# Halves of 128 slots with an expert each, constants of the attention tiles from GpSimd, and unpaced scatters of the first set, in a macaron block on one core

## The reference

```python
x = x + 0.5 * ffn(layernorm(x))       # mixture of experts, 8 experts, 2 per token
x = x + attention(layernorm(x))       # 16 heads of 8 features, causal, softmax
x = x + 0.5 * ffn(layernorm(x))

# ffn: probs = softmax(flat @ gate_w.T); the 2 best experts of a token, weights scaled to sum 1
h1 = einsum('nd,ehd->neh', flat, w1)
h3 = einsum('nd,ehd->neh', flat, w3)
y = einsum('neh,edh->ned', silu(h1) * h3, w2)     # 256 hidden features an expert
out = einsum('ned,ne->nd', y, combine)            # combine is zero outside the 2 experts
```

## Time and profile before

| | |
|---|---|
| median of 3 runs | 617.2 us (616.16 to 620.45) |
| the profiled execution's own time | 616.21 us |
| its span, first to last instruction | 613.7 us |
| mean granted TensorE clock | 0.973 |
| busy, share of the span: PE, PEld, DVE, ACT, POOL | 84%, 68%, 61%, 51%, 42% |
| matmul records | 7286 |
| DMA | 72.15 MB, 124981 packets, mean 118 GB/s |

### The profile page before, as it was taken

One profiled execution on the slowest core, in us unless ns is written; L12 is line 12 of the kernel. 1 busy time (PEld: TensorE's weight loads), 2 busy tenths in 40 slices (PEclk: granted clock), 3 DMA queues, 4 the chain that ended last, 5 costly groups with the idle time before them and its releaser, 6 DMA issues.

```text
span 613.7 us, 19025 instructions
## 1 busy us (share of the span) xinstructions
PE 514.6 (84%) x7286; PEld 416.7 (68%) x7286; DVE 373.7 (61%) x995; ACT 310.0 (51%) x597; POOL 257.5 (42%) x322
## 2 busy tenths in 40 slices
PE   2779859999998588888889886769689899999995
PEld 1667848889987355555556554546368789989994
DVE  5633933343355868989899988666356333356665
ACT  5843523344334256666666764555554234345543
POOL 7565364630563133433341111454614530555562
PEclk9999998999999589999999999998999999999999
DMA  9991297646965213746213110311134656543232
GB/s 269 307 323 35 81 277 118 137 129 146 165 153 142 80 42 95 198 126 179 90 38 97 38 55 3 123 34 33 32 79 97 138 133 130 140 131 98 67 89 56
DMA packets 124981, 72.15 MB, mean 118 GB/s; under 512 B 51936, under 2 KB 118752, under 8 KB 124896
## 3 DMA queue, kind: packets, MB, share of 16 engines
q1 hardware_dynamic: 117984, 56.78, 35.4%
q0 software_dynamic: 6912, 14.17, 9.3%
HBM read 18.88 MB, written 34.87 MB: 88 GB/s over the span
## 4 chain that ended last, share of the span: by engine, by line
PE 35%; DVE 17%; issue 4%; ACT 3%; another core or an unknown queue 2%; DMA 1%; DVEq 1%; POOL 0%; ACTq 0%; POOLq 0%
PE bank L1629 8%; DVE negmax L1310 7%; PE bank L1510 5%; PE bank L1512 5%; PE bank L1511 4%; PE bank L1742 2%; PE bank L1805 2%; ACT pt L958 2%; PE bank L1820 2%; PE bank L1772 2%; PE bank L1808 1%; PE bank L1759 1%; DVE rden L1327 1%; PE bank L1522 1%
## 5 line engine op out<-in xcount | busy, mean ns | idle before, releaser
L1197 DVE SCALAR_TENSOR_TENSOR pt<-bank,pt 128x512 f32<-128x512 f32 x122 | 84.2, 691 | 152.6 <-PE bank L1512 69.4
L708 POOL DMA_INDIRECT yg<-sorted_y,row x108 | 104.2, 965 | 146.9 <-PE bank L1629 64.2
L958 ACT ACTIVATE pt<-bank 128x768 f32<-128x768 f32 x128 | 103.8, 811 | 87.7 <-PE bank L1781 81.8
L694 POOL DMA_INDIRECT sorted_x<-xs,row x108 | 106.2, 984 | 90.0 <-DVE pt L1197 32.3
L1629 PE MATMUL bank<-w,pt 128*128 (+1 forms) x976 | 131.8, 277 | 7.6 <-issue 5.4
L1629 PEld LDWEIGHTS bank<-w,pt 128*128 128x128 f32 x976 | 119.7, 192 | 13.6 <-issue 10.0
L1310 DVE TENSOR_REDUCE negmax<-bank 128x10 f32<-128x640 f32 x128 | 104.1, 817 | 30.6 <-PE bank L1759 26.7
L841 ACT ACTIVATE pt<-bank 128x512 f32<-128x512 f32 x122 | 73.2, 600 | 57.3 <-PE bank L1512 38.9
L1742 PE MATMUL bank<-zc 63*64 63x64 f16 (+3 forms) x1024 | 44.4, 251 | 28.0 <-DVE negmax L1310 22.9
L849 ACT ACTIVATE yb<-bank 128x256 f32<-128x256 f32 x82 | 31.5, 384 | 67.9 <-PE bank L1629 43.2
L1742 PEld LDWEIGHTS bank<-zc 63*64 63x64 f16 x1024 | 19.4, 108 | 55.7 <-DVE negmax L1310 37.0
(11 more groups left out here) (171 smaller groups left out, 1014.1 us busy)
## 6 DMA issues: line engine op xcount, KB each, us to landing
sorted_y<-yb SPq DMA_DIRECT2D x82, 128.0 KB
zc<-qk_rows SPq DMA_DIRECT2D x96, 64.0 KB
sorted_x<-zeros SPq DMA_DIRECT2D x2, 2944.0 KB
qk_rows<-qksplit SPq DMA_DIRECT2D x8, 512.0 KB
sorted_x<-zeros SPq DMA_DIRECT2D x1, 2432.0 KB, 11.3
sorted_x<-zeros SPq DMA_DIRECT2D x1, 2176.0 KB, 10.2
X<-x_in SPq DMA_DIRECT2D x8, 256.0 KB, 5.3
zc<-w_up SPq DMA_DIRECT2D x8, 256.0 KB, 7.1
```

The source lines that it names most:

```text
L694: ps.indirect_dma_start(out=sorted_x[s], out_offset=bass.IndirectOffsetOnAxis(ap=row[:, s, k, t:t + 1], axis=0), in_=xs[:, R0[s] + t, :], ...
L708: ps.indirect_dma_start(out=yg[:, a % D_YG, k, :], out_offset=None, in_=sorted_y[s], in_offset=bass.IndirectOffsetOnAxis(ap=row[:, s, k, t ...
L958: s_.activation(pt[:, hg, (u % 2) * 768:(u % 2 + 1) * 768].rearrange("p (a n) -> p a n", a=2), bank[:, B_ST:B_ST + 2, 0:384], ACT.Exp, sca ...
L1197: v_.scalar_tensor_tensor(hid[:, n % D_HID], bank[:, B_H3 + n % 2, :], 1.0 / WSCALE, silu[:, n % D_H], ALU.mult, ALU.mult).then_inc(prod_d ...
```

## The change

It does three things, and moves numbers with them.

1. **Halves of 128 slots.** Each expert now starts at a new block of 128 rows, `BLK`, and a tile of 256 slots consists of two blocks that each have an expert of their own. The worst case is counted in blocks, `NB` = 31, 39, 39, 27, and a tile takes two: `NT` = 16, 20, 20, 14. `woffset` has an entry for each block. In `tile_up` each matmul of 256 columns becomes two of 128, each with the weights of its block's expert; `down`, which worked on 128 slots at a time before, takes each half's own column. Columns are still loaded four at a time, so a load now covers two tiles.
2. **Constants from GpSimd.** POOL sets `vaug` with two memsets and `zc` with four, the ones of the keys by an fp32 word whose bits are two fp16 ones (`TWO_ONES`). Two stand ahead of the first set's scatters, the other four behind them, ahead of the second set's, two of them behind a wait for `w_lo`. SP's five DMAs and their small source tiles go.
3. **Pacing.** `FREE` is 24, so no scatter of the first set waits for a product any more, and those of the second set wait for earlier units than before.

The unit numbers at which other work hangs are moved for the smaller count of units: the second group's projections from 52, 54, 56 to 47, 49, 51, its normalisation from 48 and 50 to 45 and 46, the gathers' pace, the places of the column loads.

```diff
+BLK = 128
+PER = SLOTS // BLK
+NB = tuple((2 * n * P + E * (BLK - 1)) // BLK for n in RT)
-NT = tuple((2 * n * P + E * (SLOTS - 1)) // SLOTS for n in RT)
+NT = tuple(-(-n // PER) for n in NB)
...
-            return U_TILE[3] + 2 + 9 * d // 13 if p else U_TILE[1] + 2 + 7 * d // 10
+            return U_TILE[3] + 2 + 8 * d // 13 if p else U_TILE[1] + 2 + 7 * d // 10
...
-            def blank_values():
-                row_of = value_row[:, :, :].rearrange("p a b -> p (a b)")
-                sp.dma_start(vaug[:, :, :, :, :].rearrange("p a b c d -> p (a b c d)").rearrange("p (n c) -> p n c", c=2 * D),
-                             row_of.unsqueeze(1).broadcast_to([P, 16, 2 * D])).then_inc(vaug_set, 16)
-            def blank_keys():
-                sp.wait_ge(w_lo, 9)
-                for par in range(2):
-                    for side, what in ((0, zeros), (1, ones_h)):
-                        sp.dma_start(zc[:, par, side].rearrange("p a b -> p (a b)").rearrange("p (n c) -> p n c", c=2 * D),
-                                     what[:, :].unsqueeze(1).broadcast_to([P, 16, 2 * D])).then_inc(zc_set, 16)
-            sp.wait_ge(consts, 18)
-            blank_values()
-            blank_keys()
...
+            def blank_values():
+                ps.memset(vaug[:, :, :, :, :], 0.0).then_inc(vaug_set, 1)
+                pool.wait_ge(vaug_set, 1)
+                ps.memset(vaug[:, :, :, :, DK:DK + 1], 1.0).then_inc(vaug_set, 1)
+            def blank_keys(par, side):
+                ps.memset(zc[:, par, side].rearrange("p a b -> p (a b)").bitcast(F32), (0.0, TWO_ONES)[side])\
+                    .then_inc(zc_set, 1)
-            FREE = 12
+            FREE = 24
...
-                    pool.wait_ge(prod_done, done((n - FREE) * 7 // 10, D_H))
+                    pool.wait_ge(prod_done, done((n - FREE) * 6 // 10, D_H))
...
             masks()
+            for side in range(2):
+                blank_keys(1, side)
             for t in range(RT[0]):
                 scatter(0, t, first_pace)
+            blank_values()
+            pool.wait_ge(w_lo, 9)
+            for side in range(2):
+                blank_keys(0, side)
             for t in range(RT[1]):
...
-                        cols = bass.ds(columns[s][i] + c * P, P)
-                        last = split_product(bank[:, b0 + n % 2, c * SLOTS:(c + 1) * SLOTS],
-                                             wh[:, cols], wl[:, cols], x[:, 0], x[:, 1])
+                        for v in range(PER):
+                            cols = bass.ds(columns[s][PER * i + v] + c * P, P)
+                            toks = slice(v * BLK, (v + 1) * BLK)
+                            c0 = c * SLOTS + v * BLK
+                            last = split_product(bank[:, b0 + n % 2, c0:c0 + BLK],
+                                                 wh[:, cols], wl[:, cols], x[:, 0, toks], x[:, 1, toks])
...
-                                         w2[:, bass.ds(offset + c * D, D)], start=u + c == 0, stop=c == 1,
+                                         w2[:, bass.ds(offsets[u] + c * D, D)], start=u + c == 0, stop=c == 1,
...
-                    if b == ROUTED + 2:
+                    if b == ROUTED + 2 or b == ROUTED + 3 and u < 2:
                         weight_columns(2, PIECE)
...
-                if slot >= NT[0] - 8:
+                if slot >= LAG + 5:
                     weight_columns(1, PIECE)
```

More of the change, by code:

```diff
@@ L52 @@
 WSCALE = 256.0
+TWO_ONES = 2.0 ** -7 * (1.0 + 15.0 / 8192.0)
 EPS = 1e-5
@@ L140, in build_macaron @@
         zeros = sb("zeros", [P, 2 * D], F16)
-        ones_h = sb("ones_h", [P, 2 * D], F16)
-        value_row = sb("value_row", [P, 2 * D // 32, 32], F32)
-        bounds = sb("bounds", [P, E, ETILES], F32)
+        bounds = sb("bounds", [P, E, EBLKS], F32)
         before = sb("before", [P, E, E], F32)
-        tile_no = sb("tile_no", [P, NTMAX, E - 1], F32)
+        tile_no = sb("tile_no", [P, PER * NTMAX, E - 1], F32)
         stats = sb("stats", [P, TILES, 6], F32)
@@ L171, in build_macaron @@
         chosen = sb("chosen", [P, RTMAX + 1, E], BF16)
-        over = sb("over", [P, E, ETILES], F32)
+        over = sb("over", [P, E, EBLKS], F32)
         ntiles = sb("ntiles", [P, E], F32)
@@ L330, in no_use @@
             eng.sem_inc(count, 1)
-        CONSTS = 22
+        CONSTS = 19
         block = ctx.enter_context(nc.Block())
@@ L1143, in places @@
                 total = bank[:, B_M0, n * E:(n + 1) * E]
-                link(v_.tensor_tensor(over[:, :, :], total.unsqueeze(2).broadcast_to([P, E, ETILES]),
+                link(v_.tensor_tensor(over[:, :, :], total.unsqueeze(2).broadcast_to([P, E, EBLKS]),
                                       bounds[:, :, :], ALU.is_gt))
@@ L1151, in places @@
                 v_.scalar_tensor_tensor(place[:, 0:n, :],
-                                        start[:, :].unsqueeze(1).broadcast_to([P, n, E]), float(SLOTS),
+                                        start[:, :].unsqueeze(1).broadcast_to([P, n, E]), float(BLK),
                                         bank[:, B_M0, 0:n * E].rearrange("p (a b) -> p a b", b=E),
@@ L1581, in weight_columns @@
             def weight_columns(s, count=None):
-                i0 = len(columns[s])
-                i1 = min(NT[s], i0 + (count or NT[s]))
+                i0, end = len(columns[s]), PER * NT[s]
+                i1 = min(end, i0 + (count or end))
                 if i0 == i1:
                     return
-                base = Y_TILE[s] - (Y_SECOND if s >= SECOND else 0)
+                base = PER * (Y_TILE[s] - (Y_SECOND if s >= SECOND else 0))
                 regs = [column_regs[(base + i) % COLUMNS] for i in range(i0, i1)]
@@ L1623, in tile_up, with down @@
                         between()
-            def down(n, offset):
+            def down(n, offsets):
                 pe.wait_ge(prod_done, done(n, D_H))
@@ L1640, in tile_down @@
                 pe.wait_ge(y_copied, freed(Y_TILE[s] + i))
-                down(U_TILE[s] + i, columns[s][i])
+                down(U_TILE[s] + i, columns[s][PER * i:PER * (i + 1)])
             def dense_down(p, n):
@@ L1650, in dense_down @@
                     pe.wait_ge(w2_loaded[e // 2], 16)
-                down(U_DENSE[p] + n, e * HID)
+                down(U_DENSE[p] + n, [e * HID] * PER)
             def experts(s, beside=None):
```

38 lines of the change are left out of this document (17 added, 21 removed).

## The result

The changed kernel took **659.7 us** (median of 5 runs, 659.46 to 664.97) beside 617.65 for the kernel before (5 runs, 616.16 to 622.95): ratio **1.067, 95% interval 1.063 to 1.072**. I had forecast 610, with a range of 586 to 622. The profiled execution took 664.97 us, with a span of 663.2. In the changed kernel `split_product` is lines 1505 to 1507, `down` 1627, the scatter 683, the column load 1585.

A forecast was written before the change was run, and what follows sets the result against it. PE bounds the routed stages, its sequencer now setting the tile time. Terms -8.2 - 26.4 + 24.9 - 3 + 8.5 - 7.3 + 3 = -8.5, +1 for attention's `zc` rows, gave 610 us, range 586 to 622.

The forecast's parts named there:

- part 1: Constant stores as GpSimd memsets, scatters unpaced: PE's stall before the first routed tile goes, at no cost, -8.2 us.
- part 6: Work between routed tiles hides in the array's idle time, -7.3 us; against it, late sequencer deliveries lie bare, +3 us.
- The stall at the first tile: PE's 10.04 us step before the first routed tile falls to 2.20, and the next unit gives 0.3: -8.2 us.
- Fewer tiles: Six routed tiles fewer in each block, at 2.20 us each: -26.4 us.
- A tile on the array: 24 products of 128 columns take 1.34 us for 1.31, a tile 2.23 us: the array is no obstacle.
- A tile in the sequencer: 22 register and semaphore instructions at 0.117 us each make a routed tile 2.57 us, over the array's 2.23: +24.9 us.
- Column loads: 35 loads of weight columns for 22, 0.53 us each, partly bare beside routed tiles and in attention: +8.5 us.
- The sequencer's lead: Where a routed stage begins, PE's sequencer is ahead, which hides its time once more: -3 us (2 and 1).
- (b): Rival: with the lead gone, sequencer hiccups lie bare in routed tiles, 0.25 us each, 16 us for 3: 623 us, chance 0.12.
- (a): Rival: the array stays the bound in routed tiles, because register instructions overlap: 587 us, chance 0.12.
- (c): Rival: weight loads pace the short products, a tile 3.3 us: 655 us, or 632 if half overlapped, chance 0.02.
- (d): Rival: the first tile's stall stays, because unpaced scatters crowd their own landing: +8, 618 us, chance 0.04.

The follow-up runs named there:

- a1: The changed kernel as it is, run again in a session at level 580: 580.2 us beside 580.5 for the kernel before, ratio 1.000.
- b1: The kernel before with the memsets and the changed pacing, without the halves, at level 620: 651.9 us beside 623.6, ratio 1.045.
- b3: The changed kernel with `FREE` put back from 24 to 12, at level 620: 643.7 us in one run, beside 623.6 for the kernel before.
- b4: The changed kernel as it is, at level 620: 665.6 us in one run, beside 623.6 for the kernel before.
- a4: The kernel before as it is, run for its trace at level 580: 580.7 us in one run.
- e4: The changed kernel with one weight column for both halves of a tile (another output), at level 580: 552.3 us beside 581.1, ratio 0.951.
- c1: The kernel before with the memsets alone, old pacing and tiles, at level 580: 571.4 us beside 580.1, ratio 0.986.

## Why the prediction was wrong, and where it was right

**The step that failed** is in part 1: "So the stall goes with 9 us to spare, even if the scatters gain nothing", with the cost of the unpaced scatters set at nothing. I priced the pacing only by when the last scatter would be through. At level 620, on which the comparison stands, it also kept POOL's DMAs apart, and without that PE's first routed tile took 23.8 us, and two other units took 10 us each. The second set's scatters, which I had through by 130 even at worst, ended at 147 (at 113 in a1). By stage the changed kernel lost 21 us in A, where I had it 8 ahead, and 13 in B. Its partner is part 6, "a third or so: +3 us" for late deliveries of the sequencer: I had seen one of 1.04 us and scaled it with the count of instructions. It does not scale with them: b1, with the old count of instructions, has the same drip, and b3 and b4 show that 22 us of the loss depend on POOL's pacing.

**How much of the 42 us is what.** At level 580 the change is worth nothing (a1). At level 620 putting `FREE` back is worth 22 (b4 less b3, one run each), and 20 remain (b3 less the kernel before). By stages b3 lies above the first trace of the kernel before by 6 in A, 9 in B, 1 in C, 8 in D and 7 in E (31 for 20, in the main since that trace is of a run at 616.2, and in b3's session the kernel before took 623.6). Behind 100 us they are waits for issue of at most 1.3 us each, 14 us of them ahead of L1627 alone. Most of the 8 and 7 in D and E comes with the halves (and the places of loads and gathers that moved with them): b1, without them, has only 2 and 1 there (99.4 and 50.8). How halves, memsets and the remaining scatters share A and B no run at that level shows, and why the halves cost 7 us among dense units, whose own products did not change, is open too. So with the failed step put right the forecast would still have missed at this level.

**The terms, against a1 and a4** (level 580, where nothing else disturbs):
- The stall at the first tile: -8.2 forecast, -10.5 in A, and -8.7 to -10.6 in three pairs of runs. Right. Both `zc` memsets take 1.8 us each and `vaug` 3.5, inside the bounds, and cost nothing.
- Fewer tiles, -26.4: right in kind. e4, which has them without the register instructions, is 15.5 us below c1 in B and D; 64 tiles of 2.29 for 2.20 take 5.8 back, and its second set's first tile starts some 5 late.
- A tile on the array: 2.23 forecast, 2.29 measured (e4).
- A tile in the sequencer: 2.57 forecast, 2.65 measured, 0.120 us an instruction for 0.117. Right in kind: 64 tiles at 0.45 over the old 2.20 are +29 us and swallow the 26.4 of the fewer tiles. On the forecast they are 64 x 0.08 = +5.
- Column loads: 0.53 us each forecast. The ten of set 1 have distances of 3.10 to 3.70, 3.35 in the mean, 0.69 over 2.66 (+6.9 for 5.3); the seven of set 3 0.60 (+4.2 for 3.7).
- The sequencer's lead: -3 forecast. Four tiles of 2.23, 2.29, 2.29 and 2.45 are -1.3, in the first block only.
- Sum with what was measured: -7.5 - 2.3 + 5.1 + 2.1 + 1.7 = -0.9. Measured: -0.3 in the medians (ratio 0.996 to 1.003), -2.7 over the stages of the two traces. So at this level the forecast was 7 us too good, most of it the 0.003 us an instruction and the bare loads.

**The rivals.** (b), late deliveries that lie bare, had the right kind of loss and the right sign, but it let them come with the count of instructions, at most 0.25 us a tile; what came was 24 us in one tile, so its 623 was far too low as well, and its chance of 0.12 too small. The bound was taken from a trace in which the pacing was on, and the change took just that away. (a) and (c) fall with a1 and e4: the changed tile takes 2.65, the array gives 2.29 when the sequencer does not hold it up, and in a1 24 short products in a row, from 76.65 to 77.94, start 0.056 us apart. By the 81 ns for a pair of weight load and product that the Trainium skill gives (TensorE: Matmul & The Clock Gate, section Back-to-back issue gap) a tile would take 2.83, an estimate. The 2.29 of e4 and the 0.056 of a1 do not agree with it. (d) falls: the transposes were issued at 65.9, and PE never waited for them.

**What I had said would show it.** Ends of tiles 2.5 to 2.6 apart with "issue": 2.65, yes. No wait for `pt<-sorted_x`: yes. The second routed stage as long as before within 3 us: +3.9 at level 580, +6.8 in the first comparison. The first score product at 189 to 191: no, it starts at 232.1 in the first comparison; at level 580 it came 7.4 us earlier than before (180.7 for 188.1), the distance that this sign meant (198.2 before). Dense units at 2.20: yes between waits, but E grew by 8.1 us in the first comparison.

**Left open.** What puts a session on one level or the other. Whether memsets or pacing alone make drips at level 620, and whether one pause ends the first (the runs meant for it fell on the other level). Why the same row of scatters has no drip beside it until 58.89. That what is late is PE's instruction fetch is an inference: the profile shows only that PE waits for nothing else, that the starts come in steps of 0.7 us, and that the stretches end when POOL's DMAs pause. And one form of it can be ruled out, packets of instructions that come late one by one. Queue 8 of the page, which brings instructions, has 69 packets of 16 KB, one for some 255 of PE's 17617 recorded instructions. They take 0.9 to 1.5 us, 1.11 in the mean, and 1.09 in a1 at level 580; the long drip has one, at 93.8, and the next starts at 123.3, after its end.

## What to carry to other kernels

A wait that only seems to slow an engine down may be what keeps its DMAs apart: before it goes, ask what else the burst behind it will meet, not only whether the burst is through in time. Compare two kernels in more than one session, for a difference of 7% can belong to one level of the machine and be nothing on the other. And count register instructions beside matmuls: where each tile has its own dynamic address, ten more of them (1.2 us of sequencer, 2.20 to 2.65 us a tile) take back the work that finer tiles save.

## What the runs showed of the hardware

- All kernels of a session stand on one level, and the levels are 6 to 7% apart for the kernel before (580, and 618 to 624) and 14 to 15% for the changed one (580, and 660 to 666). The gap depends on the kernel: the two kernels are equal at one level and 42 us apart at the other.
- At level 620, PE's instructions start 0.7 us apart or a multiple of it for up to 24 us, while GpSimd issues an indirect DMA every 1.26 us (not beside every such row: there is none until 58.89 beside the 24 from 32.07 on); in the three traces read for it the drip near 90 us ends 3.2 to 4.6 us after the last of these. At level 580 the same 22 DMAs in a row do nothing to it.
- An instruction on registers or semaphores costs PE's sequencer 0.12 us (24 in 2.80 us before; 22 in a tile of 2.65 us now), though the profile records those of the products as 32 to 51 ns. A load of four registers is recorded as 0.33 us and costs its tile 0.6 to 0.7.
